# The recurrence of a selective state space as one scan instruction a state, steps side by side, in a two-layer image kernel

## The reference, cut to what matters

```python
xz = einsum('nld,ed->nle', seq, in_proj_w); xi, z = split(xz, 2)      # 32 inner channels each
xc = silu(conv1d(xi) + conv1d_b)                                        # 4 taps over the 8 steps
dt, Bm, Cm = split(einsum('nld,ed->nle', xc, x_proj_w), [1, 17])        # 16 states
dt = softplus(dt * dt_proj_w + dt_proj_b)
dA = exp(dt[..., None] * A)                       # (n, 8, 32, 16)
dBx = dt[..., None] * Bm[:, :, None, :] * xc[..., None]
def step(h, inp):
    a, b, c = inp
    h = a * h + b
    return (h, sum(h * c[:, None, :], axis=-1))
ym = (ys + D * xc) * silu(z);  out = einsum('nld,ed->nle', ym, out_proj_w)
```

## Time and profile before

| what | value |
|---|---|
| median of 2 runs | 12652.6 us (12647.89 to 12657.32) |
| profiled execution | 12655.08 us, span 12653.3 us |
| mean granted TensorE clock | 0.879 |
| busy: PE, DVE, ACT, POOL | 10473.0, 9662.9, 6718.3, 3459.2 us |
| first and last L1274 start | 4805.3 and 12280.6 us |

### The profile page before, as it was taken

One profiled execution on the slowest core, in us unless ns is written; L12 is line 12 of the kernel. 1 busy time (PEld: TensorE's weight loads), 2 busy tenths in 40 slices (PEclk: granted clock), 3 DMA queues, 4 the chain that ended last, 5 costly groups with the idle time before them and its releaser, 6 DMA issues. The chain is left out here.

```text
span 12653.3 us, 157712 instructions
## 1 busy us (share of the span) xinstructions
PE 10473.0 (83%) x48832; PEld 4882.2 (39%) x48832; DVE 9662.9 (76%) x10054; ACT 6718.3 (53%) x10685; POOL 3459.2 (27%) x2546
## 2 busy tenths in 40 slices
PE   5888888888888887888888888888888888888880
PEld 3444444444444442333333333333333333333330
DVE  6666667766676667888888888888888888888874
ACT  4455455555454545555555555555555555555543
POOL 2222222222222222233332333333233333323320
PEclk9999999999999997888888888888888888888885
DMA  2222222222222221000000000000000000000019
GB/s 56 57 67 57 68 64 66 67 64 62 57 57 67 57 58 27 18 17 17 19 17 18 17 17 19 17 18 17 17 19 18 17 17 18 18 18 17 17 26 231
DMA packets 807490, 504.05 MB, mean 40 GB/s; under 512 B 603504, under 2 KB 705904, under 8 KB 802896
## 3 DMA queue, kind: packets, MB, share of 16 engines
q1 hardware_dynamic: 703824, 344.89, 12.1%
q0 software_dynamic: 49152, 100.76, 2.2%
q10 hardware_dynamic: 54016, 51.91, 1.4%
HBM read 109.27 MB, written 103.81 MB: 17 GB/s over the span
## 5 line engine op out<-in xcount | busy, mean ns | idle before, releaser
L1050 POOL TENSOR_TENSOR b_hh<-b_crep,b_hh 128x1024 f32<-128x1024 f32 x1000 | 2341.2, 2358 | 5375.2 <-ACT b_crep L1090 5029.4
L1398 PE MATMUL b_rep<-b_bcs,b_pick 96*128 96x512 bf16 x6400 | 2379.0, 474 | 788.8 <-DVE b_hh L1254 502.0
L1418 PE MATMUL b_acc<-b_hh,b_ident 128*128 128x512 f32 x6400 | 2918.4, 594 | 0.0
L1254 DVE TENSOR_TENSOR b_hh<-b_rep,b_uu 128x1024 f32<-128x1024 f32 x1600 | 1884.3, 1219 | 1005.9 <-PE b_rep L1398 992.4
L231 POOL DMA_DIRECT2D kvsel<-kv x1536 | 1106.0, 722 | 3456.4 <-issue 2624.1
L1274 DVE TENSOR_TENSOR b_tmp<-b_dA,b_hh 128x1024 f32<-128x1024 f32 x1400 | 1713.3, 1224 | 41.3
L1277 DVE TENSOR_TENSOR b_hh<-b_tmp,b_hh 128x1024 f32<-128x1024 f32 x1400 | 1711.6, 1223 | 34.5
L1418 PEld LDWEIGHTS b_acc<-b_hh,b_ident 128*128 128x128 f32 x6400 | 1210.0, 190 | 1362.7 <-issue 1305.2
L1090 ACT ACTIVATE b_crep<-b_rep 128x1024 f32<-128x1024 f32 x1000 | 979.8, 1028 | 1387.4 <-PE b_rep L1398 1386.3
L1398 PEld LDWEIGHTS b_rep<-b_bcs,b_pick 96*128 96x128 bf16 x6400 | 515.4, 106 | 2681.4 <-DVE b_hh L1254 1418.4
L1143 ACT ACTIVATE b_dA<-b_pre,b_negA 128x896 f32<-128x896 f32 x1600 | 1544.9, 1036 | 2.4
(11 more groups left out here) (148 smaller groups left out, 12371.8 us busy)
## 6 DMA issues: line engine op xcount, KB each, us to landing
kvsel<-kv SPq DMA_DIRECT2D x1600, 64.0 KB, 2.0
kvsel<-kv POOLq DMA_DIRECT2D x1536, 64.0 KB, 2.0
xpad<-in_x SPq DMA_DIRECT2D x18, 1568.0 KB, 10.6
ys<-ysb ACTq DMA_DIRECT2D x16, 1600.0 KB, 9.4
b_yc<-ys SPq DMA_DIRECT2D x100, 256.0 KB, 2.7
b_bcs<-b_hi SPq DMA_DIRECT2D x400, 64.0 KB, 2.0
b_bcs<-b_mid SPq DMA_DIRECT2D x400, 64.0 KB, 2.0
b_bcs<-b_lo SPq DMA_DIRECT2D x400, 64.0 KB, 2.0
```

Of the source, the lines that this page charges most:

```text
L1050: nc.gpsimd.tensor_tensor(out=now, in0=crep[:, q % CREPS, :], in1=now, op=ALU.mult).then_inc(s_pm, 1)
L1254: nc.vector.tensor_tensor(out=hh[:, h, i, :], in0=rep[slot % 2][:, :], in1=uu[:, :], op=ALU.mult).then_inc(s_use, 1)
L1398: m = nc.tensor.matmul(rep[s % 2][:, HT * j:HT * (j + 1)], pick[:, i], bcs[:, of, block_, HT * j:HT * (j + 1)], start=True, stop=True)
L1418: m = nc.tensor.matmul(acc[:, HT * j:HT * (j + 1)], ident[:, :], hh[:, 1 - h, i, HT * j:HT * (j + 1)], start=False, stop=(h == 0 and i == ...
```

## The change

The columns of a chunk change their order: the 8 steps of a sequence lie side by side (column 8m + t for sequence m and step t). The recurrence of one state is then one `tensor_tensor_scan` over 1024 columns, which computes state = decay x state + input from column to column. `dA` gets all 1024 columns; its step 0 is set to zero once, so that each sequence starts afresh. `xc` and `zs` are written in the new order out of PSUM by ACT; `decay` writes steps 1 to 7 of each sequence; `project` takes every eighth column of `ym` as weights. `tmp` is gone, and `crep` has two buffers.

```diff
-        CREPS = 3
+        CREPS = 2
...
-        dA = sb("dA", [C, 2, HALF, TOK - C])
+        dA = sb("dA", [C, 2, HALF, TOK])
...
+        def later(x):
+            return x.rearrange("c (m t) -> c m t", t=T)[:, :, 1:T]
...
-        STEPS = 2 * (T - 1)
+        STEPS = HALF
...
-                    nc.scalar.activation(xc[:, par, h:T:2, :], misc[1 - h][:, :].rearrange("c (q m) -> c q m", m=C),
+                    nc.scalar.activation(xc[:, par, :, h:T:2], misc[1 - h][:, :].rearrange("c (q m) -> c m q", m=C),
                                          ACT.Silu, bias=v("c1b")).then_inc(s_xe, 1)
...
-                    nc.scalar.activation(zs[:, par, h:T:2, :], misc[h][:, :].rearrange("c (q m) -> c q m", m=C),
+                    nc.scalar.activation(zs[:, par, :, h:T:2], misc[h][:, :].rearrange("c (q m) -> c m q", m=C),
                                          ACT.Silu).then_inc(s_ze, 1)
...
-                    nc.scalar.activation(dA[:, h, i, :], dt[:, C:TOK], ACT.Exp,
+                    nc.scalar.activation(later(dA[:, h, i, :]), later(dt[:, :]), ACT.Exp,
                                          scale=negA[:, HALF * h + i:HALF * h + i + 1]).then_inc(s_a, 1)
...
+            nc.vector.memset(dA[:, :, :, 0:TOK:T], 0.0).then_inc(s_p1, 1)
...
                 for j in range(STEPS):
-                    t = j // 2 + 1
-                    if j > 0:
-                        dve.wait_ge(s_st, ONE + 2 * STEPS * n + STEPS * h + j)
-                    now = hh[:, h, :, C * t:C * (t + 1)]
-                    if j % 2 == 0:
-                        nc.vector.tensor_tensor(out=tmp[:, :, :], in0=dA[:, h, :, C * (t - 1):C * t],
-                                                in1=hh[:, h, :, C * (t - 1):C * t], op=ALU.mult).then_inc(s_st, 1)
-                    else:
-                        nc.vector.tensor_tensor(out=now, in0=tmp[:, :, :], in1=now, op=ALU.add).then_inc(s_st, 1)
+                    now = hh[:, h, j, :]
+                    nc.vector.tensor_tensor_scan(now, dA[:, h, j, :], now, 0.0, ALU.mult, ALU.add).then_inc(s_st, 1)
                     for f in between.get(j, ()):
                         f()
...
-                    m = nc.tensor.matmul(misc[1][:, G * K * t:G * K * (t + 1)], ym[:, C * t:C * (t + 1)], wout[:, :],
+                    m = nc.tensor.matmul(misc[1][:, G * K * t:G * K * (t + 1)], ym[:, t:TOK:T], wout[:, :],
                                          start=True, stop=True)
```

More of the change, by code:

```diff
@@ L851, in sequences @@
         NCH = NB * CHUNKS
-        CREPS = 3
+        CREPS = 2
         HT = TOK // 2
+        MH = C // 2
         vec = sb("vec", [C, NV])
@@ L870, in sequences @@
         yT = sb("yT", [C, 4, C])
-        xc = sb("xc", [C, 2, T, C])
-        zs = sb("zs", [C, 2, T, C])
+        xc = sb("xc", [C, 2, C, T])
+        zs = sb("zs", [C, 2, C, T])
         pre = sb("pre", [C, TOK])
@@ L880, in sequences @@
         bcs = sb("bcs", [3 * G * HALF, 2, 4, TOK], BF16)
-        dA = sb("dA", [C, 2, HALF, TOK - C])
+        dA = sb("dA", [C, 2, HALF, TOK])
         hh = sb("hh", [C, 2, HALF, TOK])
-        tmp = sb("tmp", [C, HALF, C])
-        wx, dtw = tmp[:, 0], tmp[:, 1]
+        spare = zs[:, 1].rearrange("c m t -> c (m t)")
+        wx, dtw = spare[:, 0:C], spare[:, C:2 * C]
         crep = sb("crep", [C, CREPS, TOK])
@@ L1218, in _ @@
             dve.wait_ge(s_w, ONE + 16 * N_W)
-            nc.vector.memset(wze[:, :, :], 0.0).then_inc(s_p1, 1)
+            nc.vector.memset(wze[:, :, :], 0.0)
+            nc.vector.memset(dA[:, :, :, 0:TOK:T], 0.0).then_inc(s_p1, 1)
             dve.wait_ge(s_p1, ONE + 1)
@@ L1236, in inputs @@
                 dve.wait_ge(s_xe, ONE + 2 * n + 2)
-                nc.vector.tensor_tensor(out=uu[:, :], in0=dt[:, :], in1=xc[:, par].rearrange("c t m -> c (t m)"),
+                nc.vector.tensor_tensor(out=uu[:, :], in0=dt[:, :], in1=xc[:, par].rearrange("c m t -> c (m t)"),
                                         op=ALU.mult).then_inc(s_u, 1)
@@ L1244, in gate @@
                     dve.wait_ge(s_o, ONE + n)
-                nc.vector.tensor_tensor(out=ym[:, :], in0=acc[:, :], in1=zs[:, par].rearrange("c t m -> c (t m)"),
+                nc.vector.tensor_tensor(out=ym[:, :], in0=acc[:, :], in1=zs[:, par].rearrange("c m t -> c (m t)"),
                                         op=ALU.mult).then_inc(s_ym, 1)
@@ L1347, in steps @@
                 nc.tensor.matmul(misc[1 - h][:, :], wdt[:, :],
-                                 xc[:, par, 4 * h:4 * h + 4, :].rearrange("c t m -> c (t m)"),
+                                 xc[:, par, MH * h:MH * (h + 1), :].rearrange("c m t -> c (m t)"),
                                  start=True, stop=True).then_inc(s_d, 1)
@@ L1405, in skip @@
                 m = nc.tensor.matmul(acc[:, HT * j:HT * (j + 1)], diag_d[:, :],
-                                     xc[:, par, 4 * j:4 * j + 4, :].rearrange("c t m -> c (t m)"),
+                                     xc[:, par, MH * j:MH * (j + 1), :].rearrange("c m t -> c (m t)"),
                                      start=True, stop=False)
```

## The result

The changed kernel took 13336.2 us (median of 2 runs, 13335.4 to 13337.0), where the kernel before took 12652.6: 1.054 times as long, with a 95% interval from 1.0495 to 1.0586. That is +684 us where I had forecast +430. The direction was right but the time lies 14 us inside the upper end of the range (13350), so a term is missing or mis-sized. The profiled execution took 13337.0 us, with a span of 13335.2.

What follows compares the result with a forecast made beforehand. No engine is full, so the order of waits decides, with PE releasing b0 and ACT's queue setting exchange A. 2.98 + 1.34 = 4.32 us a chunk over 99 chunks, 12655 + 430 = 13085 us; range 12800 to 13350.

Steps and rivals of the forecast that it cites:

- ACT's queue in A: A, the exchange behind the recurrence of states 8 to 15: ACT reaches `turned` without a pause, b6 waits 2.72 us.
- POOL's start in B: B, the exchange behind states 0 to 7: POOL's products start 0.17 us behind the recurrence's end, on DVE's last instruction.
- The scan: DVE's recurrences: a scan takes two passes, 2.29 us; the path changes by +0.2 us (B) and +0.5 us (A).
- Rivals 1 and 3: 1: scan at one pass, 12855 us, chance 0.12. 3: scan slower than two passes, at three 14800 us, chance 0.04.
- Two buffers: C rows in both exchanges: copy 2 waits for POOL's product 0; A grows by 2.98 us, B by 1.34.
- Rival 5: Third buffer hardly missed: ACT's delay absorbed before `turned`, only 1.34 and 1.5 us stay; about 12940 us, chance 0.05.
- New layout, taken at 0: Silus, decays and `project`'s loads of `ym` in steps or runs: 0 to 1 us a chunk, taken as 0.
- 1.5 us of room for b0: In A, b1 comes later at 9066.35, so b0, DVE's first `states_in` there, at 9063.70 can slip 1.5 us.
- My upper bound of 1 us a chunk: Most that the new layout's strided accesses on ACT and PE were to cost a chunk.
- My chance of 0.12 for strided reads beyond that bound: Shared with rival 2, decays slowed by runs of 7, at +0.75 us each and 13600 us.
- The sum: 2.98 + 1.34 = 4.32 us a chunk, over 99 steady chunks 428 us, giving 13085 us.
- The cachelines rule: Accesses falling on another line each time pay a penalty, lines 16 bytes in SBUF, 8 in PSUM; up to 1 us a chunk.

Runs made afterwards that it cites:

- two buffers alone: The kernel before with two buffers for C rows instead of three and nothing else: 12984.6 us, 1.0268.
- the order: Two B rows before the third C row on PE, that row's copy behind the first decays on ACT; in the kernel before 12640.3 us, in the changed kernel 12711.9 us.
- one pass: The changed kernel with a plain multiply in place of each scan, so the recurrence is not computed: 12988.8 us, 1.0272.
- order and packed `ym`: The changed kernel with the order, and with gate writing each step's columns of `ym` together so that `project` loads packed columns: 12657.4 us, 1.0009.
- spread `project`: `project`'s eight matmuls go one by one between those of `skip` and `add`; in the changed kernel, strided loads kept, 13007.5 us, 1.0283.

## Why the forecast was right in direction and short by 254 us

- *What bounds the kernel: ACT's queue in A, POOL's start in B.* Borne out where the change lengthens either (two buffers alone, +3.4 us a chunk). It is not the whole truth the other way: where the order takes these waits away, no kernel falls below 75.10 us. And a sum of waits gives a chunk only to the nearest step of 3.4 us, or of half that over two chunks; I had no such thing in the prediction.
- *The scan.* Two passes in one instruction: 2270 ns against my 2.29 us. Recurrence B takes 18.7 us (mine 18.82), A 9114.21 - 9093.25 = 20.96 (mine 21.08), DVE's busy time is 9792 (mine 9900). The Trainium skill's half throughput ("DVE: opcode table, instruction layouts, handler registers and perf-mode slots", Datapath and trigger behaviour) agrees with the trace: 2270 against 1224 ns for a pass. Rivals 1 and 3 are out.
- *Two buffers.* Mechanism, places and releasers as forecast. The term was 4.32 us a chunk, of which 0.67 are the longer recurrences (0.46 in A, 0.21 in B); the buffers alone measure 3.4 (2.42 in A, 0.99 in B), 343 us instead of 361. In the changed kernel A grows by 1.22 us behind b0 instead of 2.98, since copy 0 is late there: copy 2's wait for POOL is 1.54 us in front of it. Rival 5 is out.
- *New layout, taken at 0: the step that failed.* It measures 3.4 us a chunk, 339 us. Two things were wrong in "I take 0, because the rows with runs show nothing, and because of that room". The rows with runs are DVE's and ACT's, and no row of PE stood behind the strided loads. And the doubled `project`, which I did name as +1.9 us, was weighed against 1.5 us of room for b0 as if nothing came with it. What came with it was the clock: +1.7 us in the `add`s behind it and some 0.9 in front, together 4.5 us in front of b0 and of copy 0. My upper bound of 1 us a chunk held neither. My chance of 0.12 for strided reads beyond that bound is what widened the range; that it just holds 13336 us owes more to that than to the sum. For the Silus the bound was good: 719 and 639 ns (684 and 597 before).
- *The sum* was therefore short by 4.53 us a chunk in front of b0, and long by 1.76 behind b0 in A (2.98 against 1.22) and by 0.27 in B: +2.5 us, nearly all of the 254. The clock at the start of A (`skip` 3.62) follows the recurrences and the waits in front of it, as the kernels with one pass (2.85) and with order and packed `ym` (3.62) suggest; I had no term for it.
- *The cachelines rule* of the Trainium skill ("Advanced Engine Details and Errata", Memory Cachelines) spoke against this part, and I gave it at most 1 us. The runs agree for single elements in steps (gate 1.21 to 1.93 us, strided loads 192 to 335 ns). Runs of 7, whose neighbours share lines, cost nothing (decays at 1033 ns), and that fits the rule too.

**What stays open.** Why the chunks come in steps, and why no order goes below 75.10 us. Where the order drops a wait, PE is at 1.2 GHz for longer at the start of A (`skip` 3.46 and 3.62 us instead of 2.94), and the granted clock over two chunks is 0.84 to 0.86 in all kernels with this length. The windows of the changed kernel above read the same one chunk (81.92 us) earlier, so the clock's falls and rises recur with the chunk. That looks as if the pipeline settled where the two repeat together, but no run held the clock fixed, so it is only argued. Why the clock falls behind the strided block in every chunk in the old order and in one of two in the profiled run of the new one isn't settled either. The changed kernel with a third buffer wasn't tried.

## What to carry to other kernels

When a layout changes, list every reader of the tensor, TensorE's weight loads among them, and price each from a row of its own engine; a row of another engine is no bound. When a block on PE gets longer with small matmuls, look at the granted clock in the windows around it before calling it hidden, and try to spread the block among large matmuls. A buffer less costs what is queued behind the copy that waits; here moving that copy behind the work it held up, and its row on PE behind two B rows, was worth the whole price of the buffer (some 340 us), without a gain over the kernel that had the buffer. When several edits of unlike causes cost the same, look at the period over two or more rounds before you add terms up: where it moves in steps, a run with one edit tells whether a step was taken and not how large the delay was.

## What the runs showed of the hardware that I had not expected

- A weight load of 128x128 f32 with columns 32 bytes apart takes 335 ns instead of 192 (medians; the means are 332 and 192), so 16 of them with 64-column matmuls take 3.78 instead of 1.89 us.
- Behind such a block PE's clock fell to 1.2 GHz, though PE had no pause (0.78 and 0.65 in windows of 3 us, PE busy for all 3.00); with the same loads between 512-column matmuls it stayed at 2.4 GHz (1.00).
- DVE's write of single f32 elements 512 bytes apart took 1.93 instead of 1.21 us for 1024 of them, 0.70 ns an element. ACT's Silus that read PSUM in steps of 512 bytes and write SBUF in steps of 8 took 35 to 42 ns more for 512 elements; no run parts the two.
- Six kernels (before, and five with the new order, with or without two buffers, scans, packed `ym` and spread `project`) have chunks of 75.10 us, whatever waits they drop.
- In the profiled executions of all fourteen kernels a steady chunk, or in two of them the mean of a pair, took 75.1, 76.8, 78.5 or 81.9 us and nothing between: lengths 1.7 or 3.4 us apart.
